# A gated cross-attention block on one core: TensorE's order of scores, maxima and P.V, and the additions of the denominators

## What is computed

```python
def attention(q, k, v):              # v is the context as it is; q and k are rotated by position
    q, k = rope(q), rope(k)
    scores = einsum('bqhd,bkhd->bhqk', q, k) * scale + slope[h] * (key - query)
    return einsum('bhqk,bkhd->bqhd', softmax(scores), v)

def ffn(x):                          # act_qdq: round to 16 bits by the maximum of the whole tensor
    x = act_qdq(x)
    up, gate = act_qdq(x @ dq(w_up).T), act_qdq(x @ dq(w_gate).T)
    gate = act_qdq(gate * fixed_qdq_u16(sigmoid(gate)))
    return act_qdq(gate * up) @ dq(w_down).T     # dq: weights rounded to 4 bits in blocks of 32

x = x + tanh(g_xattn) * attention(layernorm(x), ctx, ctx)
x = x + tanh(g_ffn) * ffn(layernorm(x))
```

## Time and profile before

| | us |
|---|---|
| median of 3 runs | 1798.62 (1795.56 to 1801.59) |
| the profiled execution | 1800.73, its span 1798.9 |
| attention with its lead and tail | until about 930 |
| gate projection | 934 to 1195 |
| up projection | 1195 to 1445 |
| maximum of the product | 1447 to 1543 |
| down projection | 1545 to 1798 |

### The profile page before, as it was taken

The page is one execution under the profiler, slowest core; times in us unless marked ns, Lnnn a source line. Parts: engine busy times, 40 slices in busy tenths (PEclk is TensorE's granted clock), DMA queues, the critical chain, the costliest instruction groups (busy, mean ns, idle before and its releaser), DMA issues. The chain is left out here.

```text
span 1798.9 us, 36886 instructions
## 1 busy us (share of the span) xinstructions
PE 1605.8 (89%) x14777; PEld 633.3 (35%) x14777; DVE 1479.7 (82%) x2116; ACT 1241.8 (69%) x1974; POOL 838.6 (47%) x504
## 2 busy tenths in 40 slices
PE   3899999999999999999869999999999900699999
PEld 0233333333333333333224444444444400344444
DVE  7899999999998898898569989768889998854551
ACT  3688888888889899888723323359986699844440
POOL 5699999999999999998600100200000000000000
PEclk9999999999999999999979999999999955899999
DMA  6688888988888887776649888569973479755551
GB/s 153 151 154 179 167 164 180 177 164 167 163 173 161 171 183 151 163 151 136 139 117 275 242 250 239 203 194 284 280 226 127 139 250 302 237 189 172 176 168 61
DMA packets 344204, 331.73 MB, mean 184 GB/s; under 512 B 214849, under 2 KB 273601, under 8 KB 336097
## 3 DMA queue, kind: packets, MB, share of 16 engines
...
## 5 line engine op out<-in xcount | busy, mean ns | idle before, releaser
L1348 DVE TENSOR_REDUCE cm<-quad 128x1 f16<-128x1024 f32 x512 | 600.3, 1214 | 63.3 <-PE quad L921 62.3
L1145 ACT ACTIVATE P<-quad 128x512 f32<-128x512 f32 x1024 | 556.8, 598 | 112.3 <-PE quad L934 100.5
L1936 POOL TENSOR_TENSOR Ps<-P,P 128x2048 f32<-128x2048 f32 x93 | 441.0, 4742 | 43.2 <-ACT P L1145 43.1
L934 PE MATMUL quad<-QA,KA 101*32 101x512 f16 x4096 | 365.9, 385 | 6.8 <-ACT P L1145 5.3
L921 PE MATMUL quad<-KA,QA 100*32 100x512 f16 x4096 | 334.7, 391 | 35.6 <-DMA QA<-S 17.8
L983 PE MATMUL quad<-P,cg 128*32 128x512 f32 x2048 | 265.5, 594 | 0.0
L1010 PE MATMUL quad<-x_hl,Wu 128*128 128x512 f16 x1152 | 250.8, 381 | 3.4 <-DMA Wu<-wt_scratch 3.4
L1010 PE MATMUL quad<-x_hl,Wg 128*128 128x512 f16 x1152 | 249.3, 379 | 3.1 <-DMA x_hl<-xs 2.5
L1063 PE MATMUL quad<-Wd,oh 128*128 128x512 f16 x768 | 228.6, 379 | 0.0
L934 PEld LDWEIGHTS quad<-QA,KA 101*32 101x32 f16 x4096 | 105.0, 94 | 298.6 <-ACT P L1145 231.0
L1226 ACT ACTIVATE ev<-quad 128x1024 f32<-128x1024 f32 x96 | 97.3, 1014 | 123.4 <-PE quad L1010 117.3
...
## 6 DMA issues: line engine op xcount, KB each, us to landing
...
uf<-up_scratch SPq DMA_DIRECT2D x96, 256.0 KB, 3.6
...
xl<-in_x_dram SPq DMA_DIRECT2D x32, 256.0 KB, 5.1
```

What stands on the lines that cost most here:

```text
L934: mm = e.matmul(K.score[h % 2][j:j + 32, :], K.KA[p % 2][0:101, kt, h, j:j + 32], K.QA[p % 2][0:101, 4 * qc:4 * qc + 4, h, :], start=True, ...
L1145: e.activation(K.Pb[pb][:, h, :], K.score[h % 2], ACT.Exp, scale=SCALE / (QPOW * KPOW)).then_inc(K.a_exp, 1)
L1348: e.tensor_reduce(cm[:, col:col + 1], K.quad[UNIT["max", hm, u] % 2][:, :], AX.X, ALU.max).then_inc(K.v_max, 1)
L1936: e.tensor_tensor(K.Ps[n][:, :, :], K.Pb[(st.g - 1) % NP][:, :, :], K.Pb[st.g % NP][:, :, :], ALU.add).then_inc(K.g_sum, 1)
```

## The change

TensorE's step is written in another order: each score is followed by half a maxima tile, and P.V stands in mid-step behind the second half, except in step 1, where it comes last. The low parts are subtracted by GpSimd straight from `t1`; `copy_part` and the low parts' use of the banks are gone. GpSimd makes two additions a half, in steps 1 and 4, each with its DMA; P6 and P7 go to the ones matmuls as they are, so a half has four sets of denominators, in its steps 6 and 7 and in steps 0 and 2 of the next. P has seven buffers, in the room of one `Ps`. Each scratch tile of 512 KB is contiguous.

```diff
--- before.py
+++ after.py
@@ -26,7 +26,7 @@
 NQ = B * NH // 4
 NHALF = 2 * NQ
 LEAD = 2
-NXL, NWL, NWQ, NP = 7, 4, 2, 6
+NXL, NWL, NWQ, NP = 7, 4, 2, 7
 NXF, NXS, NEV, GW = 8, 4, 3, 1024
 NGT, NSG = 3, 2
 NUF, NUQ, NXR = 4, 3, 3
@@ -135,13 +135,13 @@
                 self.key_bias = p + 2
             elif w in (9, 12):
                 self.high = (p + 2, 1, w // 12)
-            elif w in ((10, 14) if p >= 0 else (14, 15)):
-                self.low = (p + 2, 1, w // (14 if p >= 0 else 15))
+            elif w in ((11, 15) if p >= 0 else (14, 15)):
+                self.low = (p + 2, 1, w // 15)
         if 0 <= p and p + 1 < NQ:
             if w in (0, 2):
                 self.high = (p + 1, 0, w // 2)
-            if w in (1, 6):
-                self.low = (p + 1, 0, w // 6)
+            if w in (1, 7):
+                self.low = (p + 1, 0, w // 7)
         self.side = []
 
         self.rope = None
@@ -167,13 +167,13 @@
 
 
         last, inside = hf == NHALF - 1, self.inside and hf < NHALF - 1
-        self.sum = (hf, s // 2) if last and s % 2 == 1 else (hf, {1: 0, 4: 2, 7: 1}[s]) if inside and s % 3 == 1 else None
+        self.sum = (hf, s // 2) if last and s % 2 == 1 else (hf, s // 4) if inside and s in (1, 4) else None
         self.accumulate = (hf, s // 6, s - 1) if inside and s in (3, 6) else None
         self.dens = None
-        if s == 6 and inside:
-            self.dens = (hf, 0)
-        elif s in (1, 2) and 1 <= hf < NHALF:
-            self.dens = (hf - 1, s)
+        if s in (6, 7) and inside:
+            self.dens = (hf, s - 6)
+        elif s in (0, 2) and 1 <= hf < NHALF:
+            self.dens = (hf - 1, 2 + s // 2)
         elif last and s in (3, 5, 7):
             self.dens = (hf, s // 2 - 1)
         elif hf == NHALF and s == 1:
@@ -234,8 +234,6 @@
             uses += [("max", st.hm, 2 * st.im), ("max", st.hm, 2 * st.im + 1)]
         if st.out is not None:
             uses.append(("out", st.out))
-        if st.low is not None:
-            uses.append(("part", *st.low))
     return uses
 
 
...
@@ -338,8 +341,8 @@
         self.out_rows = out.rearrange("b t c -> (b t) c")
         self.x2_d = nc.dram_tensor("x2_scratch", (N, H), F32).ap()
         self.x2r = self.x2_d.rearrange("(b i p) c -> b p i c", b=B, p=128)
-        self.gate_d = nc.dram_tensor("gate_scratch", (OT, 128, N), F32).ap()
-        self.up_d = nc.dram_tensor("up_scratch", (OT, 128, N), F32).ap()
+        self.gate_d = nc.dram_tensor("gate_scratch", (OT, N // GW, 128, GW), F32).ap()
+        self.up_d = nc.dram_tensor("up_scratch", (OT, N // GW, 128, GW), F32).ap()
         self.wt_d = [[nc.dram_tensor(f"wt{m}{j}_scratch", shape, F16).ap() for j in range(2)]
                      for m, shape in enumerate(((I, H), (I, H), (H, I)))]
 
...
@@ -421,7 +425,7 @@
 
 
         self.cg.append(A("cg3", [128, 8, 128], F32))
-        self.Pb.append(A("P5", [128, 4, 512], F32))
+        self.Pb += [A("P5", [128, 4, 512], F32), P6]
         self.xl2 = [A(f"xl2{i}", [128, H], F32) for i in range(2)]
 
 
...
@@ -523,15 +527,11 @@
     def bank_release(self, use, half):
 
         n = UNIT[use] - 2
-        while n >= 0:
+        if n >= 0:
             kind, *a = UNIT_USES[n]
             if kind == "max":
                 return self.v_max, max_no(*a)
-            if kind == "out":
-                return (self.v_x2 if half else self.v_rec), a[0] + 1
-            if half == 0:
-                return self.v_lo, part_no(*a)
-            n -= 2
+            return (self.v_x2 if half else self.v_rec), a[0] + 1
         return None
 
     def x_columns(self, n):
...
@@ -781,7 +784,7 @@
         ot, cp = n
         k = (12 * cp + ot) if dst_d is K.gate_d else 48 + 4 * ot + cp
         e.wait_ge(K.a_ev, k + 1)
-        e.dma_start(dst_d[ot, :, 1024 * cp:1024 * cp + 1024], K.ev[k % NEV][:, :]).then_inc(K.d_ev[k % NEV], 16)
+        e.dma_start(dst_d[ot, cp, :, :], K.ev[k % NEV][:, :]).then_inc(K.d_ev[k % NEV], 16)
 
     def load_wu(ot):
         if ot == 0:
...
@@ -947,42 +950,51 @@
             e.wait_ge(K.a_den, hf)
         if hf == NHALF - 1:
             e.wait_ge(K.v_sum, n + 1)
+            src = K.Ps[n % 2]
+        elif n in (1, 2):
+            e.wait_ge(K.a_exp, score_no(hf, n + 5, 3))
+            src = K.Pb[(8 * hf + n + 5) % NP]
         else:
-            if n == 1:
-                e.wait_ge(K.g_sum, sum_no(hf, n))
-            else:
-                e.wait_ge(K.d_acc[n // 2], 16 * hf + 16)
+            e.wait_ge(K.d_acc[n // 3], 16 * hf + 16)
+            src = K.Ps[n // 3]
         for h in range(4):
-            mm = e.matmul(K.den[32 * h:32 * h + 32, :], K.ones[:, :], K.Ps[n % 2 if hf == NHALF - 1 else n][:, h, :], start=n == 0, stop=n == (3 if hf == NHALF - 1 else 2))
+            mm = e.matmul(K.den[32 * h:32 * h + 32, :], K.ones[:, :], src[:, h, :], start=n == 0, stop=n == 3)
         mm.then_inc(K.pe_den, 1)
+
+    def numerators(before):
+        if before is None or not before.inside:
+            return
+        hf, kt, p = before.hf, before.s, before.p
+        if kt == 0 and hf > 0:
+            e.wait_ge(K.a_num, hf)
+        e.wait_ge(K.a_exp, score_no(hf, kt, 3))
+        for h in range(4):
+            mm = e.matmul(K.num[32 * h:32 * h + 32, :], K.cg[(p + 1) % 4][:, kt, 32 * h:32 * h + 32],
+                          K.Pb[before.g % NP][:, h, :], start=kt == 0, stop=kt == 7)
+        mm.then_inc(K.pe_pv, 1)
 
     before = None
     for st in STEPS:
         if st.inside:
             score(st.hf, st.s, 0)
+        if st.maxima:
+            row_max(st.hm, 2 * st.im, 0)
+        if st.inside:
             score(st.hf, st.s, 1)
         if st.maxima:
-            row_max(st.hm, 2 * st.im, 0)
             row_max(st.hm, 2 * st.im, 1)
-            row_max(st.hm, 2 * st.im + 1, 0)
+        if st.s != 1:
+            numerators(before)
         if st.inside:
             score(st.hf, st.s, 2)
         if st.maxima:
-            row_max(st.hm, 2 * st.im + 1, 1)
+            row_max(st.hm, 2 * st.im + 1, 0)
         if st.inside:
             score(st.hf, st.s, 3)
-
-        if st.s == 1 and st.dens is not None:
-            denominators(*st.dens)
-        if before is not None and before.inside:
-            hf, kt, p = before.hf, before.s, before.p
-            if kt == 0 and hf > 0:
-                e.wait_ge(K.a_num, hf)
-            e.wait_ge(K.a_exp, score_no(hf, kt, 3))
-            for h in range(4):
-                mm = e.matmul(K.num[32 * h:32 * h + 32, :], K.cg[(p + 1) % 4][:, kt, 32 * h:32 * h + 32],
-                              K.Pb[before.g % NP][:, h, :], start=kt == 0, stop=kt == 7)
-            mm.then_inc(K.pe_pv, 1)
+        if st.maxima:
+            row_max(st.hm, 2 * st.im + 1, 1)
+        if st.s == 1:
+            numerators(before)
         if st.out is not None:
             hf = st.out
             for half, src, sem, done in ((0, K.denT, K.a_den, K.pe_tden), (1, K.numT, K.a_num, K.pe_tnum)):
...
@@ -1122,12 +1134,6 @@
         dst = dst[:, :, 0:3:2, :] if w else dst[:, :, 0:2, :]
         e.activation(dst, src, ACT.Copy).then_inc(K.a_hi, 1)
 
-    def copy_part(p, w, half):
-        use = ("part", p, w, half)
-        e.wait_ge(K.g_rope, rope_no(p, w))
-        e.wait_ge(*K.bank_release(use, 0))
-        e.activation(K.bank(use, 0), K.t1[w][:, 4 * half:4 * half + 4, :].rearrange("t i c -> t (i c)"), ACT.Copy).then_inc(K.a_cp, 1)
-
     def exponent(hf, kt, h):
         pb = (8 * hf + kt) % NP
         n = 8 * hf + kt
@@ -1136,8 +1142,10 @@
             m = n - NP
             e.wait_ge(K.pe_pv, m + 1)
             hm, km = m // 8, m % 8
-            if hm < NHALF - 1 and km % 3 < 2:
-                e.wait_ge(K.g_sum, 3 * hm + km // 3 + 1)
+            if hm < NHALF - 1 and km >= 6:
+                e.wait_ge(K.pe_den, den_no(hm, km - 5))
+            elif hm < NHALF - 1 and km % 3 < 2:
+                e.wait_ge(K.g_sum, sum_no(hm, km // 3))
             elif hm < NHALF - 1:
                 e.wait_ge(K.d_acc[km // 3], 16 * hm + 16)
             else:
...
@@ -1357,13 +1363,8 @@
     def low_part(p, w, half):
         rows = slice(4 * half, 4 * half + 4)
         e.wait_ge(K.a_hi, part_no(p, w, half))
-        if p > 0:
-            e.wait_ge(K.d_st[w][half], stack_no(p - 1))
         dst = K.S[w][:, rows, :, :, :].rearrange("t i h n d -> t (i h) n d")
         src = K.t1[w][:, rows, :].rearrange("t i (h d) -> t (i h) d", d=HD)
-        if p > 0:
-            e.wait_ge(K.a_cp, part_no(p - 1, w, half))
-            src = K.bank(("part", p, w, half), 0).rearrange("t (g d) -> t g d", d=HD)
         e.scalar_tensor_tensor(dst[:, :, 2 - w, :], src, 1.0, dst[:, :, 0, :], ALU.mult, ALU.subtract).then_inc(K.v_lo, 1)
 
     def centre_x(n):
...
@@ -1797,6 +1799,15 @@
             else:
                 e.wait_ge(K.g_ropek, p)
             e.tensor_tensor(K.t1[w][:, :, :], K.t1[w][:, :, :], K.t2[:, :, :], ALU.add).then_inc(K.g_rope, 1)
+
+    def low_part(p, w, half):
```

(15 more changed lines are left out.)

43 lines of the change are left out of this document (24 added, 19 removed).

## The result

The changed kernel takes 1804.59 us (median of 10 runs, 1802.34 to 1805.60), the kernel before, run beside it, 1799.51 (10 runs, 1795.56 to 1801.59): ratio 1.0027, 95% interval 1.0017 to 1.0037. That is 5.1 us slower: clear of the noise by the interval, but just inside the 0.3% (5.4 us) that I had called no change. The forecast was 1811. The profiled execution has a span of 1800.5 us and a time of 1802.34; it is the shortest of the ten, and only 1.6 us above the one of before.

The account below looks back on a forecast made before the run. TensorE was taken as the bound, working 24.54 of 26.49 us a half. Attention +15.5 and scratch -2.5 made +13 on the profiled 1800.7, so 1813.7, less 2.1 for a median: 1811 us, range 1790 to 1828.

Parts of the forecast that it names:

- the likeliest case: Whole kernel: attention halves lengthen through an added denominator set and bank round trips; 1803 to 1824 us, chance 0.58.
- forecast case: Whole kernel: a median of 1803 to 1824 us, around the forecast of 1811; chance 0.58.
- Fourth D, 0.86 us: TensorE in attention: four sets of denominators a half instead of three, not hidden, +0.86 us a half.
- Waits taken off, 1.80: TensorE in attention: of 1.95 us of waits a half, all but the step 6 DMA wait go, -1.80 us.
- Waits added, 1.60: TensorE in attention: the new order adds waits for score banks, evictions, reductions and the DMA, 1.60 us a half.
- Times 31: Attention: a half goes from 26.49 to 27.0 us, +0.5, over 31 halves +15.5 us.
- Low parts on GpSimd, 0: GpSimd in attention: two low parts of 1.69 us a half replace an addition of 4.59, no time change.
- Seventh P buffer, 0: ScalarE in attention: with seven buffers P6 and P7 can be held without delaying it, 0 us.
- Contiguous scratch, -2.5 (ends -8 and +2): Feed-forward loads: mostly hidden by busy TensorE in the up projection, gain at most behind it; -2.5 us, ends -8 and +2.
- the first: Attention: added waits don't come and old ones stay gone, nearly no change; 1793 to 1802 us, chance 0.2.
- The third, GpSimd late: GpSimd in step 1: a low part delays the first addition, denominators wait, +25 us more, about 1837; chance 0.08.

Follow-up runs that it names:

- e2: The changed kernel with the strided scratch of the kernel before; 1812.51 us, ratio 1.0055 to 1.0079 to the kernel before.
- e9: The kernel before with contiguous scratch and the low parts moved to GpSimd, old order and three additions kept; 1854.15 us, ratio 1.0143 to 1.0279.
- e1: The kernel before with the contiguous scratch alone; 1791.95 us, ratio 0.9937 to 0.9960 to the kernel before.

## Why the prediction was right and wrong

The range (1790 to 1828) held, and in the attention the mechanism of the likeliest case is what the traces show. The sign was right and the size was not: +12.4 us was forecast from 1798.6 to 1811, +5.1 came. That 1804.59 still lies in the forecast case (1803 to 1824), and over the 1804 to which I gave 0.63, is luck: the kernel before, run beside it, was 0.9 us above the 1798.62 from which I had set these bounds, while the attention cost less and the layout gave more than I had said. By the steps of the prediction:

- **Fourth D, 0.86 us.** Right. The matmuls against ones are 1024 now where they were 776, so 31 sets of eight more, and 407.17 to 408.02 is 0.85.
- **Waits taken off, 1.80.** Right for what it named: in the changed kernel there is no D in step 1, and the M's of steps 7, 0 and 1 lose 0.02 or less each (before: 0.2 to 0.35). The D behind the accumulating DMA loses 0.06, not 0.15.
- **Waits added, 1.60.** Right, 1.70 in all: S0 and S1 behind steps 3 and 5 0.30 + 0.26 (forecast 2 x 0.28), step 1 0.36 + 0.13 (0.54), T and M in steps 4 and 5 0.38 (0.35), the rest in small pieces. The 0.38 is split otherwise than I had it: T loses 0.33 of it, all in the first 20 halves, and M 0.05. Half 27.0 forecast, 27.09 measured.
- **Times 31.** Wrong in size. The half of before that it is set against is 26.66 and not 26.49 in the first 28 halves, and the last three don't have the pattern. +11.9 instead of +15.5; with start and end of the attention +11.4. e2 measures this part by itself as 12.6.
- **Low parts on GpSimd, 0.** Right here (1.37 us each, below my 1.69), and e9 shows what it hangs on: the addition that goes.
- **Seventh P buffer, 0.** Right: between 100 and 800 us ScalarE's exponentials wait for scores alone.
- **Contiguous scratch, -2.5 (ends -8 and +2).** This is the step that failed most. e1 and e2 measure -8.0 and -7.9, at the end that I had set as a bound. My reason was that "loads that land earlier are hidden" while TensorE is busy 240.94 of 250 us. The overlap was wrong: TensorE waited 3.4 us for weights that the queue, held up by gate tiles, issued late, and lost another 1.7 at the lower clock. The list of waits of that stage, which I didn't read, names them. The busy share could not: 5.7 of the 9.06 us that are missing lie behind the end of the projection, and over the projection itself TensorE was busy 98.7% (250.84 of 254.20). I also took the price from the 256 KB loads of `up_scratch`, which don't get shorter.

With -8 in place of -2.5 and +11.4 for the attention, the same sum gives 1800.7 + 11.4 - 8 - 2.1 = 1802.0 for a median, 2.6 under the measured 1804.6. With medians alone, 1799.51 + 12.6 - 8.0 = 1804.1: the +11.4 comes from single profiled runs, and that of the changed kernel is 2.25 us under its median.

The Trainium skill (DMA: Bandwidth & Descriptors, the table entry on HBM row pitch at large powers of two) gives 207 GB/s at a pitch of 512 KiB, where its full rate is 214, for copies of tiles with 16 KiB a partition between HBM tensors. Carried over to a pitch of 16 KiB, the layout would be worth nothing. The runs here don't agree with that: from a pitch of 16 KiB to one of 4 KiB the 512 KB loads go from 5.1 to 4.4 and from 5.8 to 5.3 us, and the time falls by 8 us. The measurement decides. The page names lock-stepped streams on one HBM channel as a possible cause; no run here shows whether it is one here.

Of the rivals, the first (1793 to 1802, 0.2) came near in time but for another reason: the waits came as forecast, and the layout gave its 8. The third, GpSimd late, did not happen in the changed kernel; in e9, with three additions, it did.

What is open: why a transposing and an accumulating DMA stall each other for some 30 us, whether the coincidence or the place makes it, and why rows 16 KiB apart load more slowly.
